# The sync queue's order in a cross-attention stage: the row store goes last, two waits on TensorE's progress go

## What is computed

```
x = x + gamma * attention(q = layernorm(x), k = v = context)   # 8 heads, head size 64, softmax over 512
n = layernorm(x)
shared = (silu(n @ sw_gate) * (n @ sw_up)) @ sw_down           # inner size 1408
p = softmax(n @ router_w.T); the two largest of 8, rescaled to sum 1
routed = sum over those two experts of w * ((silu(n @ w_gate[e]) * (n @ w_up[e])) @ w_down[e])   # inner size 352
out = x + routed + sigmoid(n @ shared_gate_w) * shared
```

## Time and profile before

| | us |
|---|---|
| median of 3 runs | 927.85 (922.9 to 928.9) |
| the profiled execution, time | 931.65 |
| its span | 929.9 |
| TensorE busy | 863.5 |
| VectorE busy | 570.5 |
| ScalarE busy | 505.5 |
| GpSimd busy | 442.8 |

### The profile page before, as it was taken

One profiled execution on the slowest core, in us unless ns is written; L12 is line 12 of the kernel. 1 busy time (PEld: TensorE's weight loads), 2 busy tenths in 40 slices (PEclk: granted clock), 3 DMA queues, 4 the chain that ended last, 5 costly groups with the idle time before them and its releaser, 6 DMA issues.

```text
span 929.9 us, 13754 instructions
## 1 busy us (share of the span) xinstructions
PE 863.5 (93%) x4624; PEld 715.8 (77%) x4624; DVE 570.5 (61%) x819; ACT 505.5 (54%) x862; POOL 442.8 (48%) x422
## 2 busy tenths in 40 slices
PE   4988898988986999999999999999999999999993
PEld 3666666666665888888888888888889999999992
DVE  4987888888762553442121212113989999999991
ACT  3886788778754332112111111112778888888881
POOL 5464666677450000004333000000589999999983
PEclk9998999999997999999999999999999999999996
DMA  9112223133234331400032002553945343434442
GB/s 104 47 35 86 85 80 135 57 113 113 80 125 136 103 102 46 136 1 1 2 136 25 1 0 91 187 187 105 336 103 91 69 89 69 83 75 83 76 68 35
DMA packets 63236, 81.24 MB, mean 87 GB/s; under 512 B 15369, under 2 KB 34825, under 8 KB 63186
## 3 DMA queue, kind: packets, MB, share of 16 engines
q1 hardware_dynamic: 53426, 60.14, 21.2%
q0 software_dynamic: 9760, 20.49, 12.3%
HBM read 53.01 MB, written 27.60 MB: 87 GB/s over the span
## 4 chain that ended last, share of the span: by engine, by line
PE 74%; POOL 11%; issue 7%; DVE 3%; ACT 2%; DMA 2%; POOLq 0%; SPq 0%; DVEq 0%; ACTq 0%
PE scores L1359 9%; PE scores L1360 9%; PE scores L1361 9%; PE bank L1373 4%; PE bank L1374 4%; PE bank L1375 4%; PE scores L1224 3%; PE bank L1459 3%; PE bank L1460 3%; PE bank L1461 3%; PE scores L1435 3%; PE scores L1437 3%; PE scores L1436 3%; PE bank L1435 3%; PE bank L1437 2%
## 5 line engine op out<-in xcount | busy, mean ns | idle before, releaser
L1016 DVE TENSOR_TENSOR sg<-scores,sg 128x512 f32<-128x512 f32 x44 | 30.4, 692 | 218.4 <-PE scores L1361 202.6
L1359 PE MATMUL scores<-x_hl,wsp 128*128 128x512 f32 x352 | 138.1, 392 | 0.0
L1360 PE MATMUL scores<-x_hl,wsp 128*128 128x512 f32 x352 | 137.8, 391 | 0.0
L1361 PE MATMUL scores<-x_hl,wsp 128*128 128x512 f32 x352 | 137.5, 391 | 0.0
L615 POOL DMA_INDIRECT slot_rows<-msrc,posi x32 | 36.1, 1129 | 184.6 <-PE scores L1361 178.2
L630 POOL DMA_INDIRECT xg<-x_normed_rows,meta x39 | 39.3, 1007 | 160.0 <-PE scores L1383 141.7
L789 ACT ACTIVATE sg<-scores 128x512 f32<-128x512 f32 x44 | 26.3, 598 | 160.2 <-PE scores L1361 160.2
L936 DVE TENSOR_TENSOR ptl<-bank,pth 128x512 fp32r<-128x512 f32 x128 | 87.7, 686 | 27.2 <-ACT pth L690 26.7
L690 ACT ACTIVATE pth<-bank 128x512 fp32r<-128x512 f32 x128 | 76.7, 599 | 43.2 <-PE bank L1233 42.5
L684 ACT ACTIVATE pb<-scores,negmax 128x512 f32<-128x512 f32 x128 | 88.1, 694 | 13.0 <-DVE negmax L926 13.0
L796 ACT ACTIVATE hh<-sg 128x512 fp32r<-128x512 f32 x44 | 27.8, 632 | 115.9 <-DVE sg L1016 100.9
(11 more groups left out here) (175 smaller groups left out, 2235.4 us busy)
## 6 DMA issues: line engine op xcount, KB each, us to landing
wex<-in_L_ffn_w_gate SPq DMA_DIRECT2D x8, 704.0 KB, 4.3
wex<-in_L_ffn_w_up SPq DMA_DIRECT2D x8, 704.0 KB, 6.1
xb<-in_x SPq DMA_DIRECT2D x16, 256.0 KB, 3.5
cn<-in_ctx SPq DMA_DIRECT2D x16, 256.0 KB, 3.0
x_rows<-xb SPq DMA_DIRECT2D x16, 256.0 KB, 2.0
x_normed_rows<-x2n SPq DMA_DIRECT2D x16, 256.0 KB, 2.3
x_normed_transposed<-x2T SPq DMA_DIRECT2D x16, 256.0 KB, 3.2
x_hl<-x_normed_transposed SPq DMA_DIRECT2D x4, 1024.0 KB, 5.2
```

Of the source, the lines that this page charges most:

```text
L1359: te.matmul(bk[:, :], hi, xhi, start=(h == 0), stop=False)
L1360: te.matmul(bk[:, :], hi, xlo, start=False, stop=False)
L1361: ins = te.matmul(bk[:, :], lo, xhi, start=False, stop=(h == HC - 1))
```

## The change

In the sync engine's step the store of x2's rows goes from the first place to the last of the recurring DMAs, and both waits on TensorE's transposes (`paced`) are taken out, with the helper. All data waits stay, and so do all DMAs. No other engine's program is changed.

```diff
-            def paced(t, n):
-
-                if there(t):
-                    sp.wait_ge(e_t, 8 * t + n)
-
             def step(i):
-                if there(i - 1):
-                    store_rows(i - 1)
                 if there(i - 3):
                     store_normed(i - 3)
                 if there(i + 2):
-                    paced(i - 1, 8)
                     load_values(i + 2)
                 if there(i - 3):
                     store_columns(i - 3)
                 if there(i + 4):
-                    paced(i, 3)
                     load_x(i + 4)
+                if there(i - 1):
+                    store_rows(i - 1)
                 if i == 7:
                     load_block(0, 0)
                 if i == NT - 4:
```

## The result

The changed kernel takes 896.93 us in the median (896.45 to 899.08, 4 runs) against 925.38 of the kernel before (920.69 to 928.9, 4 runs), a ratio of 0.970 with an interval of 0.9647 to 0.9753. That is 28.5 us less, where 26.5 were forecast; the time itself was forecast at 901.3, from the 927.85 that three runs of the kernel before had given.

What follows compares the result with a forecast made beforehand. GpSimd's ring, with its DMA wait for the context tile, bounds the loop; 9 x 13.9 + 4 x 14.35 = 182.5 us replaces 209.0, a gain of 26.5, so 927.85 - 26.5 = 901.3 us, range 892 to 912.

Steps and rivals of the forecast that it cites:

- The ring through GpSimd and the context tile: Attention loop: GpSimd, TensorE's scores and VectorE's `att` form a closed chain of 15.67 us per step, 3.25 of it DMA wait.
- The waits on transposes: Sync queue: the two `paced` waits, ahead of the loads of `cn` and x; their removal was costed at nothing.
- the first wait: Sync queue: wait for all 8 transposes of tile i-1; costs nothing alone, but would hold the load once the store moved.
- The step's floor: Nine plain loop steps: they end at 13.9 us, where TensorE's gaps of 1.76 us are closed.
- VectorE's bound of 13.3: Plain loop steps: VectorE's busy time of 13.27 us, taken as the lower bound of the step.
- The four steps of `first_tokens`: Loop steps i = 9 to 12: two more GpSimd instructions keep GpSimd the bound, at 14.35 us a step.
- The clock: Three loop steps of 19.62, 17.23 and 17.36 us, where TensorE's clock fell, were counted at full clock after the change.
- the low stretch: TensorE's fall from 2.4 to 1.2 GHz in three loop steps, said to come of GpSimd's wait, 5.6 us at longest.
- Another ring: Loop: VectorE, ScalarE and TensorE hand-overs of `pth` and `ptl` set steps of 14.8 us; 911 us, chance 0.12.
- a late load: Sync queue: `store_normed` or other transfers hold the `cn` load over 11 us, so the wait stays; 928 us, chance 0.05.
- a falling clock: Loop: TensorE's clock falls in each step, 1.5 us a time, 19.5 us longer than forecast; 921 us, chance 0.04.
- The collision of GpSimd and VectorE: Loop: GpSimd's earlier instructions collide with VectorE's work, 1.5 us each, three a step; 946 us, chance 0.03.

Runs made afterwards that it cites:

- e1: Kernel before with the store of x2's rows moved last, both waits on TensorE's transposes kept: 898.91 us, ratio 0.9718.
- e3: Kernel before with only the load of the context tile moved ahead of the row store, without its wait on transposes: 899.43 us, ratio 0.9728.
- e2: Kernel before with both waits on TensorE's transposes taken out, the store left first: 925.71 us, ratio 1.0008.
- e5: Changed kernel with the load of the context tile put behind the row store: 913.94 us, ratio 0.9891 to the kernel before.
- e7: Changed kernel with both norm statistics reading 64 of 512 columns, giving VectorE less work: 898.59 us, ratio 0.9716 to the kernel before.
- e8: Changed kernel with two of the three score products, giving TensorE less work: 891.87 us, ratio 0.9639 to the kernel before.
- e4: Changed kernel with GpSimd's `first_tokens` moved from behind the residual to behind `kl`, where GpSimd waits for VectorE: 894.77 us, ratio 0.9681 to the kernel before.
- e6: Changed kernel with two more GpSimd additions of 128 x 512 between `xn` and `kh` in every step: 917.15 us, ratio 0.9913 to the kernel before.

## Why the prediction was right

*The bound.* The ring through GpSimd and the context tile, and the store at the queue's head as the cause of the late load: right. e1 and e3 remove the wait by two different edits, e2 and e5 keep it or bring it back by two others.

*The waits on transposes.* Costed at nothing, and e2 measures nothing. The remark that the first wait, left in with the store moved, would "be what holds the load" is true and costs nothing: it holds it for 3.6 us, but there were 11 to spend, and e1 is as fast.

*The step's floor.* 13.9 us were taken, 13.6 came; that term was mis-sized by 0.3 x 9 = 2.7 us, and it is most of what the loop gave beyond the forecast (29.6 against 26.5). The 13.9 was TensorE's busy time beside its gaps, and busy time depends on the gaps. In the changed kernel's timeline the four transposes of probabilities ahead of `x2n`'s are listed with 0.66 us, but the next group starts 0.49 behind them:

```profile
109.81 0.66 PE L1226 MATMUL bank<-ident,pb 128*128 128x128 f32 x4
110.30 0.60 PE L1260 MATMUL bank<-ident,x2n 128*128 128x128 f32 x4
```

Ahead of a gap the full 0.66 counts, in flow only 0.49. The kernel before has these rows around its two gaps, beside those of the earlier trace rows:

```profile
110.03 0.66 PE L1233 MATMUL bank<-ident,pb 128*128 128x128 f32 x4
...
112.22 0.48 PE L1247 MATMUL bank<-pth,vs 128*128 128x512 f32 x1
...
113.44 0.40 PE L1249 MATMUL bank<-ptl,vs 128*128 128x512 f32 x1
```

and the changed kernel, in flow:

```profile
110.66 0.48 PE L1240 MATMUL bank<-pth,vs 128*128 128x512 f32 x1
...
111.87 0.40 PE L1242 MATMUL bank<-ptl,vs 128*128 128x512 f32 x1
112.20 0.50 PE L1217 MATMUL scores<-kh,qh 64*128 64x512 f32 x2
```

At the first gap the two groups count 0.66 and 0.41 (111.81 to 112.22) against 0.49 and 0.36, at the second one product counts 0.40 against 0.33: together 0.29 of the 0.30. That is worked out from these rows of one step; no run tests it by itself. Which engine is the floor was right (e7, e8), with VectorE's bound of 13.3 close under it, where e8 finds 13.1.

*The four steps of `first_tokens`.* 14.35 forecast, 14.28 measured, and e4 shows that their place in the ring is the reason.

*The clock.* Counted at full speed in the three steps that fell: right, 1.00 in all 13. The reason given, that the low stretch "comes of the wait itself", is only half borne out. In the kernel before the clock fell in a step (168.42 to 185.65) whose wait was shorter than the 3.25 us of the step of the earlier trace rows, which kept 1.00:

```profile
173.14 0.61 POOL L541 CAST kh<-cn 128x512 fp32r<-128x512 f32 x1 [2.07 <-DMA cn<-in_ctx]
```

And e5, with its gaps still there, kept 1.00 throughout. What holds is that in the loop the clock fell only in kernels whose TensorE waits for GpSimd in every step: the kernel before, e2, and e6, where the gaps are opened again and it falls in two steps. Of a step's 94 matmuls 44 are transposes, and with hardly a gap between them the granted clock stayed at 1.00. The Trainium skill (TensorE: Matmul & The Clock Gate, Part 4: PE-mode transpose) says that transposes don't count as TensorE's being busy in the same way as other matmuls; in this mix, beside 50 other matmuls, no loss by it is seen.

*The rivals.* Another ring (911), a late load (928), a falling clock (921): none is in the trace. The collision of GpSimd and VectorE (946) neither: `x2n` took 0.766 us in the mean of the loop against 0.767, though it now meets other work of VectorE's:

```profile
L545 POOL TENSOR_SCALAR x2n<-xb,rstd,nmr 128x512 f32<-128x512 f32 x13 | 10.0, 766 | 0.0
```

*What is luck.* The front's 3.1 us are in the profiled difference and not in the forecast's reach; the medians, 28.5 and 25.8 us apart on two chips, enclose 26.5. The forecast was read off an execution 6.3 us above the median, with three falls of the clock in its loop, and taken from the median whole. How many falls a median execution has no run shows (e2's profile, with the same steps, has two), so part of the agreement within 2 us may be chance. Of the 4.4 us between the forecast time and the measured one, 2.5 are the median of the kernel before, which a fourth run lowered from 927.85 to 925.38.

## What to carry to other kernels

In a queue that issues in order, ask of each wait at its head which transfers behind it could already run; a load whose buffer is long free must not stand behind a store that waits for the newest result, least of all if the engine that makes that result wants the load next. The gain of taking such a wait away isn't the wait (3.25 us here) but the distance to the next bound (2.1), so list the gaps that the next engine has. Its busy time is a first estimate of the new step and a little too long here (13.9 against 13.6), since part of it closes with the gaps. Where some steps carry extra work in the same ring, look for the idle place that the new schedule opens in that engine, and put it there.

## What the runs showed of the hardware

The same load took 3.07 us from issue to use in a burst of five transfers (the kernel before) and 2.66 us with one other (e5). GpSimd's addition of a 128 x 512 float32 tile to itself took 1.04 us (e6), that of two tiles 1.28. TensorE's clock fell in three of the loop's 13 steps in the kernel before, in two in e2 (17.15 and 17.68 us, granted 0.90) and in two in e6 (17.10 and 17.19), and in none of e5's, though TensorE waits in all of these kernels. What decides among steps that look alike stays open. At the start of an execution the matmuls' durations changed from 0.63 to 0.40 us at 15 us in some profiles and not before 24 us in others, the same kernel included, and the rows' granted clock didn't always show it.
